# Row scores of unmasked cross attention streamed three times, and matmuls of constants where the plan has TensorE wait

## What is computed

```python
x = _L0_xcond_ref(x, cond, ctx, ...)   # masked self attention with rope, cross attention (masked), MLP, all gated
x = _L1_xcond_ref(x, ctx, cond, ...)   # cross attention alone, queries of x, keys and values of the normed context
x = _L2_xcond_ref(x, cond, ctx, ...)   # self attention, cross attention, MLP
x = _L3_xcond_ref(x, cond, ctx, ...)   # self attention with rope, cross attention with rope, MLP

def _attn(q, k, v):
    scores = jnp.einsum('bqhd,bkhd->bhqk', q, k) * scale
    return jnp.einsum('bhqk,bkhd->bqhd', jax.nn.softmax(scores, axis=-1), v)
```

## Time and profile before

| | |
|---|---|
| median of 3 runs | 2699.41 us (2697.4 to 2700.83) |
| the profiled execution | 2701.83 us, span 2700.0 us |
| TensorE matmul busy | 2581.8 us, 96% of the span |
| VectorE busy | 1747.8 us, 65% |
| ScalarE busy | 1445.8 us, 54% |
| granted TensorE clock, mean | 0.968 of 2.4 GHz |

### The profile page before, as it was taken

How to read it: one execution, slowest core, us unless ns; L and a number is a source line. 1 busy time by engine, 2 the same in 40 slices (tenths; PEclk the granted TensorE clock), 3 DMA queues, 4 the chain that set the end, 5 groups by cost and what they waited for, 6 DMA issues and landing times.

```text
span 2700.0 us, 54860 instructions
## 1 busy us (share of the span) xinstructions
PE 2581.8 (96%) x19774; PEld 1869.2 (69%) x19774; DVE 1747.8 (65%) x4179; ACT 1445.8 (54%) x2421; POOL 667.4 (25%) x650
## 2 busy tenths in 40 slices
PE   7789999999999999989999999999999999999987
PEld 5557767677677766656777777777777777777765
DVE  4466666666665556677677767676677666766632
ACT  1235555544545555544566655556565656555642
POOL 2022222222221222212222222223323232324220
PEclk9799999999999988888999999999999999999989
DMA  6343423433433465554443434334335343434310
GB/s 206 101 146 123 128 94 120 133 96 100 139 105 108 132 200 167 167 174 142 132 146 112 144 109 135 119 124 134 118 103 177 101 139 106 144 100 136 105 62 18
DMA packets 297860, 340.55 MB, mean 126 GB/s; under 512 B 72954, under 2 KB 188506, under 8 KB 297020
## 3 DMA queue, kind: packets, MB, share of 16 engines
q1 hardware_dynamic: 264124, 286.68, 34.2%
q10 hardware_dynamic: 33280, 50.35, 5.1%
q0 software_dynamic: 192, 0.01, 0.0%
HBM read 203.42 MB, written 116.21 MB: 118 GB/s over the span
## 4 chain that ended last, share of the span: by engine, by line
PE 79%; DVE 10%; issue 3%; DMA 2%; SPq 1%; POOL 1%; ACT 1%; ACTq 0%; DVEq 0%; POOLq 0%
PE gen L1356 13%; PE gen L1365 12%; PE gen L1252 12%; PE gen L1218 11%; PE gen L1336 11%; PE score L1280 4%; PE score L1265 4%; PE score L1310 4%; DVE row_max L1691 4%; PE score L1294 3%; PE score L1316 3%; PE gen L1227 3%; DVE xhat L1605 1%; DVE x L1742 1%; POOL xnT L1550 1%
## 5 line engine op out<-in xcount | busy, mean ns | idle before, releaser
L1691 DVE TENSOR_REDUCE row_max<-score 128x4 f32<-128x1024 f32 (+1 forms) x640 | 650.6, 1045 | 210.4 <-PE score L1280 130.1
L1508 ACT ACTIVATE probs<-score 128x1024 f32<-128x1024 f32 (+1 forms) x576 | 570.9, 1026 | 369.6 <-PE score L1310 251.9
L1356 PE MATMUL gen<-xnT,w_w1M 128*128 128x256 f32 x1536 | 373.5, 392 | 3.1 <-ACT xnT L1446 2.9
L1365 PE MATMUL gen<-w_w2M,hT 128*128 128x256 f32 x1536 | 355.7, 385 | 3.0 <-ACT hT L1532 2.4
L1365 PEld LDWEIGHTS gen<-w_w2M,hT 128*128 128x128 f32 x1536 | 286.7, 191 | 65.1 <-issue 26.2
L1356 PEld LDWEIGHTS gen<-xnT,w_w1M 128*128 128x128 f32 x1536 | 284.9, 192 | 59.4 <-issue 7.5
L1550 POOL TENSOR_TENSOR xnT<-xnT,xhat 128x512 f32<-128x512 f32 x112 | 148.9, 1330 | 707.0 <-DVE xhat L1720 706.8
L1542 POOL TENSOR_TENSOR rstd<-var_eps,minus_half 128x2 f32<-128x2 f32 x160 | 115.7, 723 | 809.2 <-DVE var_eps L1599 809.0
L1532 ACT ACTIVATE hT<-gen,b_b 128x256 f32<-128x256 f32 x384 | 159.1, 472 | 179.0 <-PE gen L1356 178.0
L1446 ACT ACTIVATE xnT<-gen,mod_all 128x256 f32<-128x256 f32 x288 | 146.8, 569 | 153.7 <-PE gen L1227 151.2
L1336 PE MATMUL gen<-probs,v_self 128*32 128x256 f32 x3072 | 206.3, 386 | 0.5 <-ACT probs L1508 0.5
(11 more groups left out here) (160 smaller groups left out, 4050.4 us busy)
## 6 DMA issues: line engine op xcount, KB each, us to landing
q_stack<-parts_scratch SPq DMA_DIRECT2D x336, 256.0 KB
parts_scratch<-parts ACTq DMA_DIRECT2D x160, 256.0 KB, 2.5
parts_scratch<-parts SPq DMA_DIRECT2D x160, 256.0 KB, 2.3
k_self<-parts_scratch SPq DMA_DIRECT2D x144, 256.0 KB, 4.1
k_cross<-parts_scratch SPq DMA_DIRECT2D x192, 78.0 KB, 2.5
x_scratch<-x SPq DMA_DIRECT2D x48, 256.0 KB, 3.2
x_in<-x_scratch SPq DMA_DIRECT2D x48, 256.0 KB, 2.8
gate<-gates_scratch SPq DMA_DIRECT2D x80, 128.0 KB, 3.2
```

Source lines behind the costliest of these rows:

```text
L1356: mm = pe.matmul(buf[:, i * S:i * S + S], w["M"]["w1"][:, fc, col:col + P], xnT[s][:, fc, :], start=fc == 0, stop=fc == FC - 1)
L1365: mm = pe.matmul(buf[:, 0:D], hT[:, j, c * P:c * P + P], w["M"]["w2"][:, j, :], start=j == 0, stop=j == FFC - 1)
L1508: act.activation(probs[st.probs][0:keys, :, :], score[st.fill.buf][0:keys, :, :].rearrange("p a (r q) -> p (a r) q", r=2), ACT.Exp, bias=k ...
L1691: dve.tensor_reduce(dst, src, AX_X, ALU.max).then_inc(max_done[b], 1)
```

## The change

An unmasked cross `S` matmul now writes three copies of its 78 columns next to each other (234 columns), by a moving operand that is read three times; the next matmul of the same buffer overwrites the copies that are not its own. What VectorE reads is as before.

The planner also counts, ahead of each TensorE step that takes a bank, how long TensorE stood idle in the plan although the bank was free. It puts 0.8 of that time, divided by 0.216 us and at most 16, as matmuls of two constants (the identity and a cosine table, 128 by 256) into the step's own bank (`keep_busy`, L1226 to L1237 of the changed kernel). These are issued after the wait for the bank and ahead of the wait for the step's inputs; the step then overwrites them.

```diff
+REPEATS = 3
+FILLER, FILL, MOST = 0.216, 0.8, 16
...
+                if eng == "pe" and st.takes:
+                    freed = [st.prior[ring].end for ring in ("gen", "score") if st.prior.get(ring)]
+                    st.fillers = min(MOST, int(FILL * (now - max([busy[eng]] + freed)) / FILLER))
...
+                def keep_busy(st):
+
+                    wait_emptied(st)
+                    if not tables_known:
+                        tables_known.append(st)
+                        pe.wait_ge(tables_ready, 1)
+                    out = gen[st.buf][:, 0:S] if "gen" in st.takes else score[st.buf][:, 0, 0:S]
+                    for _ in range(st.fillers):
+                        pe.matmul(out, ident[:, :], cosT[:, :], start=True, stop=True, skip_group_check=True)
...
-                                    mm = pe.matmul(buf[:, t, at_col:at_col + CTXP], queries[rows, column(2 * u + i), c * P:c * P + P],
-                                                   keys[rows, column(2 * u + i), :], start=not blk.mask, stop=True, skip_group_check=True)
+                                    stationary, moving = queries[rows, column(2 * u + i), c * P:c * P + P], keys[rows, column(2 * u + i), :]
+                                    if blk.mask:
+                                        mm = pe.matmul(buf[:, t, at_col:at_col + CTXP], stationary, moving, start=False, stop=True, skip_group_check=True)
+                                    else:
+                                        out = buf[:, t, at_col:at_col + REPEATS * CTXP].rearrange("p (r k) -> p r k", r=REPEATS)
+                                        mm = pe.matmul(out, stationary, moving.unsqueeze(1).to_broadcast([64, REPEATS, CTXP]),
+                                                       start=True, stop=True, skip_group_check=True)
...
                 for st in plan.order["pe"]:
+                    if st.fillers:
+                        keep_busy(st)
```

More of the change, by code:

```diff
@@ L159, in __init__ @@
         self.buf = self.n = None
-        self.early = False
+        self.early, self.fillers = False, 0
         self.prior, self.got, self.times = {}, {}, {}
@@ L475, in run @@
                 continue
-            left -= 1
+            left, st.end = left - 1, now
             for ring in st.gives:
@@ L1194, in _ @@
                 pe.wait_ge(init_done, 1)
-                loaded = {}
+                loaded, tables_known = {}, []
                 def wait_weights(st):
@@ L1200, in wait_weights, with wait_emptied @@
                         pe.wait_ge(*weights_loaded(st.blk))
[L1202 to L1207, removed]
+                def wait_emptied(st):
+                    if "gen" in st.takes:
+                        if st.n:
+                            pe.wait_ge(gen_moved[st.buf], st.n)
+                        return
                     before = st.prior["score"]
@@ L1213, in fill_scores, with fill @@
                             pe.wait_ge(exp_done[st.buf], before.done)
-                    return score[st.buf]
+                def fill(st):
+                    if not st.fillers:
+                        wait_emptied(st)
+                    return gen[st.buf]
+                def fill_scores(st):
+                    if not st.fillers:
+                        wait_emptied(st)
+                    return score[st.buf]
+                def keep_busy(st):
+                    wait_emptied(st)
+                    if not tables_known:
[4 more added lines that the diff above has]
+                        pe.matmul(out, ident[:, :], cosT[:, :], start=True, stop=True, skip_group_check=True)
                 def project(out, xT, weight, cols):
```

## The result

| | before | changed |
|---|---|---|
| median of 19 executions each | 2696.36 us (2685.19 to 2703.84) | 2704.83 us (2695.56 to 2709.66) |
| ratio to before, 95% interval | | 1.0025 [1.0016, 1.0034] |
| the profiled execution, its span | 2701.83, 2700.0 us | 2702.06, 2700.3 us |
| its granted clock | 0.968 | 0.985 |

By the ratio the changed kernel is slower by a quarter of a per cent, 6.7 us. The two profiled executions hide that: they are equal within 0.3 us.

A forecast was written before the change was run, and what follows sets the result against it. TensorE was taken to bound the kernel, busy for 96% of the span, partly at half clock. The terms 0 - 10 + 7 + 3 = 0, from 2701.8 less 2.4 us, gave 2699 us, range 2677 to 2718.

The forecast's parts named there:

- Fillers are twice as long as planned: All 139 fillers: one is two instructions and 0.43 us, not 0.216, so 60 us in all and not 30.
- The last jobs, +3: Last jobs: 75 fillers, 32.4 us, against waits filled and clock given back: about +3 us, bounds -3 and +10.
- L2 and L3, +7: L2 and L3: 6.6 us for longer score steps at full clock, and one filler: +7 us.
- L0's start, 0: L0's start: 35 fillers outlast their waits by 7.4 us, clock and VectorE's waits make up for it: 0, bounds -5 and +6.
- L1, -10 by the clock's 21: 970:1345: columns and fillers cost 11 us, fewer half-clock stretches give back 21: net -10 us, bounds +11 and -38.
- seven falls: 970:1345: seven of 11 clock falls come behind row scores, followed by 54.8 us of half clock; columns were to prevent them.
- The start of the sum: The whole kernel: the profiled execution's 2701.8 us, taken as 2.4 us above the median of the runs, so 2699.4.
- D: Score steps: columns are not hidden, 0.25 us per step, +48 us in all: 2738 us; chance 0.03.
- C: L1: the clock falls stay, 10 us or less comes back; with 5 us back +16, 2715 us; chance 0.22.
- A: Whole kernel, the forecast itself: clock gains in 970:1345 are eaten by columns and long fillers, 2690 to 2708; chance 0.45.
- B: L1: the clock falls nearly all vanish, clock above 0.97, 30 us and more back for 11: sum -19, 2680; chance 0.25.

The follow-up runs named there:

- fill_short: The whole change with its 139 fillers, each of 128 columns instead of 256: 2685.68 us, ratio 0.9952 to the kernel before.
- fill_right: The whole change with a filler priced at 0.432 us instead of 0.216, so 58 fillers instead of 139: 2683.24 us, ratio 0.995 to the kernel before.
- fill_only: The change without the extra columns (78 in all row scores), all 139 fillers kept: 2703.93 us, ratio 1.0031 to the kernel before.
- fill_tail: The kernel before plus only the change's 75 fillers ahead of L3 steps, 78 columns everywhere: 2701.55 us, ratio 1.0011.
- cols_l23: The kernel before with 234 columns in the row scores of L2 and L3 alone, no fillers: 2701.84 us, ratio 1.0013.
- fill_l0: The kernel before plus only the change's 35 fillers ahead of L0 steps, 78 columns everywhere: 2702.75 us, ratio 1.0011.
- cols_l1: The kernel before with 234 columns in the row scores of L1 alone (64 steps), no fillers: 2692.54 us, ratio 0.9978.
- fill_l1: The kernel before plus only the change's 29 fillers ahead of L1 and L2 steps, 78 columns everywhere: 2698.53 us, ratio 1.0003.
- cols_only: The change without fillers, 234 columns in all unmasked cross row scores: 2695.49 us, ratio 0.999 to the kernel before.
- right_tail: The kernel before plus fillers ahead of L3 steps alone, priced at 0.432 us, 78 columns everywhere: ratio 0.9973.

## Why the forecast of no change was wrong

- **Fillers are twice as long as planned**: right, 278 instructions in place of 139. With the length or the number halved the loss turns into a gain (`fill_short`, `fill_right`). I made it a term of a balance, and expected the balance to be even. The fillers' own share of my sum is about +8 (0 in L0, some +5 in L1, +3 in the last jobs), and `fill_only` has +8.4: that side was sized right.
- **The last jobs, +3**: right in sign and size, +1.8 in the pair of traces and 1.0011 (+3) by `fill_tail`, whose interval touches none. The steps came out as worked: at 2647 sixteen fillers stand for 6.9 us where before waited 3.34.
- **L2 and L3, +7**: 0.08 us for a score step followed by other work, and nothing for one followed by scores, was right where it can be seen (0.07 to 0.08 for a single step, 0.07 for a pair, above), but only a third to a half arrives at the end: +2.2 in the pair, 1.0013 by `cols_l23`. In the third stage TensorE is busy for 1249.3 us in the changed kernel and for 1246.7 before, 2.6 us more. A half-clock stretch of 3.4 us that before had at 1339 is gone from it, worth up to 1.7; so the columns cost some 4.3 us there where I had 6.6.
- **L0's start, 0**: off by some 3 to 4 us. The pair has +4.1 and `fill_l0` 1.0011, neither clear of what executions differ by: the first stage of kernels that change nothing in it came out between 838.4 (`cols_l1`) and 850.4 (`fill_l1`). I had given 6.3 us back for clocks. In the first stage before had 34 us of half clock and the changed kernel 24, so at most 5 came back in this pair: the stretch of 3.4 us at 154.7 is not gone but stands at 150, ahead of the nine fillers.
- **L1, -10 by the clock's 21**: this is the step that failed, in its size. The clock went where I said (0.93) and the pair of traces shows -7.9. But the sum started from one execution of before that had less clock than most, 0.968 against a median of 0.971 or 0.972. What an execution loses by half clock is what the change can give back, so 102.6 us of half clock was too high a figure for the usual execution. Against the 474.3 and 477.0 us that this stage takes at the usual clock, the 473.5 of the changed kernel are a gain of 1 to 4 us and not of 10. Taken by kernels, the columns of L1 give 0.22%, 6 us (2 to 10), where my terms for them come to about -15 (3.0 of price less two thirds of the clock behind seven falls, 17.5), and its fillers give nothing (1.0003): about -5 where I had -10.
- **Which part lifts the clock**: I gave the columns seven falls and the fillers one. Each part alone does nearly the same: the second stage has a clock of 0.94 in `cols_only` and in `cols_l1`, 0.93 in `fill_only` and in `fill_l1`, and 0.94 in the change that has both. So the second part bought no more clock there and brought its price all the same.
- **The start of the sum**: I took 2.4 us off for the distance of the profiled execution from the median of three. From the median of 19 it is 5.5. Counted from trace to trace the forecast of 0 looks met (+0.2), but by luck: +4.1, +2.1, -4.8 and -1.2 against the four terms cancel.
- **The sum**: parts measured apart give -6 (columns L1), +3.5 (columns L2 and L3), and +8.4 (fillers), all by their ratios: +5.9, where the change has +6.7. Each part is known to within 4 us or so, and by medians the same parts come to +0.5 where the change has +8.5, so that they add up is not shown.
- **The rivals**: D, columns that are not hidden, has fallen: by its price two steps with 234 columns would have been 0.5 us longer together, and they are 0.07. So has C, that the falls stay: the kernel is slower as C said, but 102.6 us of half clock became 54.6, and 6.7 us are not its 16. The measured time lies in A's own range; the balance that A expected to be even is not. B's clock, above 0.97 in L1, did not come either (0.93); its 2680 also leaves out the +7 and +3 of the other stages, with which 30 us back make 2690. And of the 11 falls three were left to stay by my own count of eight, not four.

Where the 20 us between the change and `fill_right` lie: 10 to 12 in the last jobs (shown twice, by stages and by times), some 7 in L0's start by a pair whose intervals overlap. What is left for L1 is within the noise. That a profile catches low-clock executions is not the rule: the profiled execution is above its kernel's median clock in `fill_right` (0.987 to 0.984), `cols_l1` (0.980 to 0.976) and `right_tail`, below it in `fill_tail` and `fill_l0`. Two low ones of before may be chance.

## What to carry to other kernels

Before filling a wait with dummy matmuls, read from the trace how long one of them takes: a float32 matmul of 256 columns was two instructions and 0.43 us, and a plan that charged half of that turned a gain of 0.5% into a loss of 0.25%, at the same granted clock. Look for the idle bracket behind the fillers: if it is gone, they have outlasted the wait. Making matmuls longer whose step hardly grows by it (0.07 us) raised the clock where it was low, and won 0.22%; where the clock was full already the same edit came out at a cost of 0.13%, with an interval that touches none. Two ways to raise the same low clock don't add up: each alone brought it from 0.89 to 0.93 or 0.94, both together to 0.94. And before a sum is made from one profile, hold its clock and time against the other executions: what can be given back was too large here because that execution had more half clock than the usual one.

## What the runs showed of the hardware that was not expected

Little was enough to raise the clock: the longer score matmuls alone gave a median of 0.977 where the kernel before has 0.971 to 0.972, 25 fillers with them 0.983, and 139 fillers 0.985. Executions of one kernel differ by some 20 us (2685 to 2704 for 19 of before, 2689 to 2713 for 34 in another series), and their time follows the granted clock: of the 34 executions of before in one series, whose clocks lie between 0.965 and 0.977, time and clock have a correlation of -0.91, 1.9 us for a thousandth.
